# Two `xt` and value buffers, one GpSimd remainder, and another order of work in a one-core transformer layer

## The reference

```
x = x + layernorm(attention(layernorm(x)))
x = x + layernorm(ffn(layernorm(x)))

attention: Q, K, V = x W_Q + b_Q, x W_K + b_K, x W_V + b_V        (per head)
           attn = softmax(Q K^T / sqrt(64));  out = sum_h attn V W_O[h] + b_O
ffn:       gate = softmax(x gate_w^T)                              (8 experts)
           out = x weight^T + 1/16 * sum_e gate[e] * lora_V[e] (lora_U[e] x)
```

## Time and profile before

| | |
|---|---|
| median of three runs | 1090.09 us (1090.06 to 1090.18) |
| the profiled execution | 1091.16 us, span 1089.3 us |
| mean granted TensorE clock | 0.979 of full speed |
| busy | PE 94%, ScalarE 84%, VectorE 83%, GpSimd 73% of the span |
| DMA | 145 MB, 57.7% of 16 engines' time on the kernel's queue |
| instruction queues | 9 packets of 0.15 MB in all, and 10 of 0.08 MB |

### The profile page before, as it was taken

The page is one execution under the profiler, slowest core; times in us unless marked ns, Lnnn a source line. Parts: engine busy times, 40 slices in busy tenths (PEclk is TensorE's granted clock), DMA queues, the critical chain, the costliest instruction groups (busy, mean ns, idle before and its releaser), DMA issues.

```text
span 1089.3 us, 28626 instructions
## 1 busy us (share of the span) xinstructions
PE 1021.8 (94%) x8550; PEld 780.2 (72%) x8550; DVE 905.9 (83%) x1630; ACT 917.7 (84%) x3207; POOL 800.1 (73%) x778
## 2 busy tenths in 40 slices
PE   8889999999999999999999999999999999999974
PEld 7767777777777777677777777777767777777743
DVE  6888888888888888888888888888888888888841
ACT  4888888889888888888888989888988888898932
POOL 3676777787777788777778777778877777877741
PEclk9899999999999999999999999999999999999977
DMA  7364566556556556556655655755655665565570
GB/s 239 85 149 108 133 152 144 121 130 142 122 136 159 127 121 146 125 122 153 147 122 125 146 121 132 159 131 122 142 129 121 149 152 122 121 149 123 128 164 11
DMA packets 59219, 145.21 MB, mean 133 GB/s; under 512 B 17216, under 2 KB 25920, under 8 KB 59200
## 3 DMA queue, kind: packets, MB, share of 16 engines
q1 hardware_dynamic: 59200, 144.99, 57.7%
HBM read 6.50 MB, written 4.19 MB: 10 GB/s over the span
## 4 chain that ended last, share of the span: by engine, by line
PE 87%; ACT 4%; issue 3%; DVE 3%; POOL 2%; ACTq 0%; POOLq 0%; DVEq 0%
PE o_ps L460 22%; PE st_ps L438 18%; PE extra_ps L476 8%; PE qk_ps L404 8%; PE qk_ps L406 5%; PE qk_ps L405 5%; PE extra_ps L334 5%; PE extra_ps L418 4%; PE extra_ps L420 3%; PE extra_ps L419 3%; PE extra_ps L497 2%; PE extra_ps L510 2%; ACT v_sb L739 2%; ACT xt_hi L705 1%; PE extra_ps L512 1%
## 5 line engine op out<-in xcount | busy, mean ns | idle before, releaser
L1516 POOL TENSOR_TENSOR probs<-probs,inv_sum 128x1024 f32<-128x1024 f32 x256 | 486.3, 1900 | 201.4 <-DVE inv_sum L1097 201.2
L724 ACT ACTIVATE probs<-st_ps,neg_max 128x256 f32<-128x256 f32 x1024 | 477.9, 483 | 32.5 <-DVE neg_max L1089 30.2
L1089 DVE TENSOR_REDUCE neg_max<-st_ps 128x4 f32<-128x1024 f32 x256 | 310.0, 1211 | 44.7 <-PE st_ps L438 35.5
L1105 DVE STREAM_TRANSPOSE probs_b<-probs 128x1024 f32<-128x1024 f32 x256 | 313.4, 1225 | 26.8 <-POOL probs L1516 26.8
L460 PE MATMUL o_ps<-probs_t,v_sb 128*64 128x256 f32 x2048 | 253.7, 390 | 7.7 <-DVE o_lo L1113 4.3
L724 ACT ACTIVATION_READ_ACCUMULATOR probs<-st_ps,neg_max 128x1 f32 x1024 | 217.9, 213 | 0.0
L460 PEld LDWEIGHTS o_ps<-probs_t,v_sb 128*64 128x64 f32 x2048 | 136.8, 138 | 89.4 <-issue 16.0
L710 ACT CAST qk_hi<-qk_ps 128x512 fp32r<-128x512 f32 x256 | 153.5, 599 | 29.7 <-PE qk_ps L406 26.1
L438 PE MATMUL st_ps<-qk_hi 64*128 64x256 f32 x1024 | 171.9, 332 | 3.8 <-POOL qk_lo L1510 1.5
L438 PE MATMUL st_ps<-qk_lo,qk_hi 64*128 64x256 f32 x1024 | 145.2, 280 | 0.0
L1510 POOL TENSOR_TENSOR qk_lo<-qk_full,qk_hi 128x512 fp32r<-128x512 f32 x96 | 123.5, 1286 | 28.1 <-ACT qk_hi L710 14.6
(11 more groups left out here) (132 smaller groups left out, 1988.6 us busy)
## 6 DMA issues: line engine op xcount, KB each, us to landing
probs_t<-probs_b SPq DMA_DIRECT2D x1024, 128.0 KB, 2.4
out<-x_all SPq DMA_DIRECT2D x31, 128.0 KB, 1.9
x_all<-in_x SPq DMA_DIRECT2D x1, 3840.0 KB, 17.3
probs_b<-in_w_v SPq DMA_DIRECT2D x1, 512.0 KB, 4.9
probs_b<-in_w_o SPq DMA_DIRECT2D x1, 512.0 KB, 6.8
probs_b<-in_w_q SPq DMA_DIRECT2D x1, 384.0 KB, 5.3
probs_b<-in_w_k SPq DMA_DIRECT2D x1, 384.0 KB, 5.9
x_all<-in_x SPq DMA_DIRECT2D x2, 128.0 KB, 3.5
```

The source lines that it names most:

```text
L724: last = nc.scalar.activation(probs[n][:, h, j, :], st_ps[p % 2][:, (2 * h + j) * T:(2 * h + j + 1) * T], ACT.Exp, bias=neg_max[n][:, h, j ...
L1089: nc.vector.tensor_reduce(neg_max[p % N_PROBS][:, :, :].rearrange("p h j -> p (h j)"), st_ps[p % 2][:, :].rearrange("p (j s) -> p j s", j= ...
L1105: nc.vector.transpose(probs_b[chunk % 2][:, :, :, 2 * NT * n:2 * NT * (n + 1), :].rearrange("p i t n q -> p n t i q"), probs[p % N_PROBS][ ...
L1516: nc.gpsimd.tensor_tensor(probs[n][:, :, :, :].rearrange("p h j s -> p (h j) s"), probs[n][:, :, :, :].rearrange("p h j s -> p (h j) s"), ...
```

## The change

- `xt_hi`, `xt_lo` and `v_sb` have two buffers each, taken in turn by batches (`turn`, `r`). `xt_high(b)` now waits for the q, k and v products of batch b-2, and `copy_v(b, ...)` for the probabilities' products of b-2.
- `POOL_LO` is `(3,)` in place of `(1, 4, 6)`: GpSimd makes one remainder of eight in a batch, VectorE seven. There is one `qk_full` buffer in place of three, and ScalarE makes one whole copy per batch.
- To make room, `x1t` is `yt`, `ut` is `u`, `squares` are `yt` and `u`, and two constants of the set-up lie in `probs_t`. Two waits follow from it: `copy_yt` waits for `z_projected` of the batch before (in place of `y_transposed`), `apply_gate` for `variance_ready[LN_Z]` (in place of `u_transposed`).
- `run` makes loops of two batches per round, since buffer numbers must be constants. Where the number of batches is odd, one body stands ahead of the loop.
- All engines' orders are written anew, in prologue, body and epilogue.

The core of the diff:

```diff
-POOL_LO = (1, 4, 6,)
+POOL_LO = (3,)
...
-        xt_hi = sb("xt_hi", [P, T], F32R)
-        xt_lo = sb("xt_lo", [P, T], F32R)
+        xt_hi = [sb(f"xt_hi{n}", [P, T], F32R) for n in range(2)]
+        xt_lo = [sb(f"xt_lo{n}", [P, T], F32R) for n in range(2)]
...
-        qk_full_sb = {p: sb(f"qk_full{p}", [P, 2 * T]) for p in POOL_LO}
-        v_sb = sb("v_sb", [P, NT, H * DH])
+        qk_full_sb = sb("qk_full", [P, 2 * T])
+        v_sb = [sb(f"v_sb{n}", [P, NT, H * DH]) for n in range(2)]
...
-            with engine.Fori(0, high - low) as step:
-                body(step + low)
+            with engine.Fori(0, (high - low) // 2) as step:
+                for n in range(2):
+                    body(2 * step + (low + n), (low + n) % 2)
...
-                after(act, qk_projected, PAIRS * b)
-                after(act, v_projected[3], b)
+                after(act, qk_projected, PAIRS * (b - 1))
+                after(act, v_projected[3], b - 1)
...
-                after(act, o_projected, PAIRS * (b - 1) + (half + 1) * (PAIRS // 2))
+                after(act, o_projected, PAIRS * (b - 2) + (half + 1) * (PAIRS // 2))
```

## The result

The changed kernel takes 1013.91 us (median of 4 runs, 1013.4 to 1014.88) against 1090.13 of the kernel before in the same rounds (1090.06 to 1090.75): a ratio of 0.9301, 95% interval 0.9285 to 0.9317. The direction was right, the size was not.

The account below looks back on a forecast made before the run. PE and its waits were taken as the bound: 32.13 less 1.19 and 0.85, plus 0.25 leftover, gave 30.35 us per batch; 29 batches -50.1, ends +1.1, so 1041 us, 4.5% faster, range 1030 to 1067.

Parts of the forecast that it names:

- Waits at the seam: Between two loop batches, PE's waits at the transpose of xn (0.76) and first query product (0.43) vanish: gain 1.1 to 1.19 us.
- Changes of kind: In PE's loop order, 22 switches between product kinds become 20 (0.4 us), three fp32 pieces get shorter (0.45): 0.85 per batch.
- the 1054 by that rule alone: Kernel time in us if only tiling-mode changes drain TensorE, without the 0.45 for fp32 pieces: batch 0.45 longer.
- Leftover waits of 0.25 a batch: In the loop, remaining PE waits given several close margins: 0.25 us added, 30.35 us per batch (30.1 to 30.7).
- Remainders moved: Per loop batch, two of three GpSimd remainders go to VectorE: ScalarE 27.5, GpSimd 22.3, VectorE 29.0 to 29.2 us busy.
- Blocks, shared tiles, the loop: In the loop, DMA transfers stay hidden, waits from shared tiles cost nothing, and the two-batch branch costs 0 (at most 4 us).
- Ends: Before batch 3's transpose +0.6 us (-3 to +4); behind scores 6 of batch 31 +0.5 us (-2 to +2).
- A: Rival: VectorE sets the loop's pace; 31.2 us per batch, 1066 us, if half its idle time stays; chance 0.13.
- B: Rival: loop code is fetched anew each round, 56 to 160 us in 14 rounds, kernel 1098 to 1200; chance 0.10.
- C: Rival: gain given back at the ends or by the DMA; 10 us more, 1051, if the first batches run badly; chance 0.07.
- D: Rival: PE's 1.19 us of waits only move to x1's transposes or scores 3; 31.3 per batch, 1068 us; chance 0.10.

Follow-up runs that it names:

- e1: Changed kernel with scores 6 ahead of the last value quarter again in the loop: period 31.11 us (+1.18), one run of 1048.85 us.
- e2: Changed kernel with the products with probabilities 6 and 7 ahead of the transpose of xn in the loop: period 30.58 us (+0.66), one run of 1031.25 us.
- e3: Changed kernel with scores 1 moved between q/k 2 and q/k 3, two more changes of kind per batch: period 30.30 us (+0.38), one run of 1022.16 us.
- e7: Changed kernel with one more unused VectorE reduction (about 0.6 us) per loop batch: period 30.32 us (+0.39), single run of 1028.72 us.
- e8: Changed kernel with two more unused VectorE reductions (about 1.2 us) per loop batch: period 30.90 us (+0.98), single run of 1040.45 us.
- e5: Kernel before with one remainder on GpSimd and seven on VectorE, PE's order and buffers as before: 1103.67 us, ratio 1.012 to the kernel before.
- e6: Changed kernel with the loops written out as straight code for all 32 batches: 1011.47 us, ratio 0.9289, period 29.93 us.
- e15: Changed kernel with the old order of set-up and batch 0, but GpSimd's order left as changed: 1020.91 us, ratio 0.9379, batch 3's transpose at 99.5 us.
- e12: Changed kernel with batch 2's transpose, first projections and first values behind scores 7 of batch 1 again, loop untouched: 1026.35 us, ratio 0.9426.
- e4: Changed kernel with one buffer for xt_hi and xt_lo in place of two: period 29.92 us, one run of 1018.53 us.
- e10: Changed kernel with value quarters 1 to 3 of batch 1 and the transpose of batch 2 moved back in the prologue: 1014.72 us, ratio 0.9299.
- e9: Kernel before with 26 small unused products where PE waits in its prologue: 1091.46 us, ratio 1.0009.
- e11: Changed kernel with the old order of set-up and first batch on four engines, GpSimd's remainder of pair 3 behind the scaling of pair 1: 1028.66 us.
- e13: Changed kernel with another end: last block transfers issued from two queues, two PSUM banks for attention, second group ahead of batch 30's gate: 1009.46 us, ratio 0.9269.

## Why the prediction was wrong, step by step

**Waits at the seam: right, 0.13 too small.** Forecast -1.1 to -1.19, and they are gone (no bracket in the timeline, e1 and e2 bring them back). The size was read from the column of idle time. PE's starts say more. Before (a value quarter, scores 6 and the last value quarter ahead of a seam, then the scores behind it):

```profile
521.94 0.50 PE L418 MATMUL extra_ps<-wv_hi,xt_hi 128*128 128x512 f32 x1
522.84 0.38 PE L438 MATMUL st_ps<-qk_hi 64*128 64x256 f32 x2
523.74 0.50 PE L418 MATMUL extra_ps<-wv_hi,xt_hi 128*128 128x512 f32 x1
...
525.81 0.39 PE L438 MATMUL st_ps<-qk_hi 64*128 64x256 f32 x2
```

A value quarter takes 0.90 from its start to the next kind's, the one ahead of the transpose 1.71 (523.74 to 525.45), so the wait costs 0.81. Scores take 0.90 (522.84 to 523.74), those ahead of the query product 1.41 (525.81 to 527.22), so that wait costs 0.51. Together 1.32 and not 1.19.

**Changes of kind: right.** What is left is 32.13 - 1.32 - 29.92 = 0.89, against 0.85. e3 measures 0.19 per change apart from all else, and the fp32 pieces with a query product behind them are shorter as forecast: transpose of `u` 0.19 in place of 0.37, of `yt` 0.19 in place of 0.34, z 0.89 (507.46 to 508.35) in place of 1.09. The 0.89 a batch is a remainder of the sum; these rows alone give 0.4 and 0.53. The Trainium skill's drain rule ("TensorEngine Tiling (Array Packing)", Key Properties) agrees with the first of these numbers and is silent on the second; the 1054 by that rule alone is ruled out for this kernel.

**Leftover waits of 0.25 a batch: wrong, they are 0.** With the 0.13 and the 0.04 above, and rounding, this makes the 0.43 between 30.35 and 29.92, 12.5 us in 29 batches. I saw margins of 0.1 to 0.6 and added a quarter of a microsecond for caution, with no row behind it. PE is busy for 29.92 of 29.92. e7 and e8 show that the caution was close to being right: VectorE has 0.2 to spare.

**Remainders moved: right, loads as forecast.** VectorE 28.8 to 29.2, ScalarE 26.9, GpSimd 22.2 to 22.7. e5 shows that this part alone gives next to nothing in the loop (-0.10) while PE's order is the old one. Whether the new order needs it is open: it was not run with three remainders on GpSimd.

**Blocks, shared tiles, the loop: right, nothing in the loop.** PE never waits there for blocks. e6 puts the loop itself at nothing measurable.

**Ends: the step that failed most.** Forecast +0.6 before the transpose of batch 3, from -3 to +4; measured -11.9. I treated the start as the old straight code with two more remainders on a VectorE that was 94% busy from 40 to 75 us, and priced only what is added. But the diff rewrites the straight code as well. VectorE idled 22 of 107.6 us before (12.7 of 95.7 after), all but 2 of it outside the window of 40 to 75 that I rested on. 1.9 of the 11.9 are the products that moved behind, as forecast. The new order of the set-up is worth about 4 (e15), and pulling batch 2's transpose, projections and values three to six groups ahead the rest (e12), both as what putting the old piece back costs, and both with a part of the clock in them. The second `xt` buffer has its share in this (e4: 3 us in one profile with a half-speed stretch at 59.9 to 63.3). Early values alone (e10) and half speed in the start of the kernel before (e9) don't explain it. Behind scores 6 of batch 31 I forecast +0.5 and it was -3.1. Nearly all of that is the clock, for which the forecast had no term. PE stands still there as long as before (21.5 us against 21.8), but it is busy for 26.9 us in place of 29.6 although it has more products (183 against 165), at a granted clock of 0.81 in place of 0.71: before the last serial chain half speed was granted for 6.8 us (973.3 to 980.1), in the kernel before for 17.1 (1046.2 to 1063.3). From the last transpose of `xn` to the end the variants with an untouched end take 76.6 to 82.8 us, the shortest (e2, e6) with 3.4 us at half speed ahead of that chain and the longest (e7, e10, e11) with 20.4.

**The rivals.** A did not happen: VectorE follows PE, though with 0.2 us to spare. B is excluded by the packets (14 and 15 on the two queues, none in 770 us of loop) and by e6. Of the two statements of the Trainium skill that were weighed there ("Runtime: NRT & Kernel Launch", Instruction fetch mechanics), the trace agrees with the buffer sizes: from the third round on no taken branch of a two-batch body brings a packet. C came with the other sign. D did not happen: no wait of PE appears at `x1` or scores 3.

## What to carry to other kernels

Straight code ahead of a loop is a kernel of its own: when a change rewrites it, lay it out like the loop, above all where the next batch's first projections start, because that is when the busiest helper engine runs dry. Here three batches of start gave 12 us and 29 batches of loop 63. Read what a wait costs from the starts of PE's groups, with the wait and without it, and not from the idle column: the column is missing the step to the next product (1.19 against 1.32). And don't add an allowance for waits that no row shows; put it in the range. Look at the DMA engines' share before adding a second issuing queue: here it was 91% already, and the queue gained 0.4 us.

## What the runs showed of the hardware that was not expected

- PE's granted clock at the ends differs between executions of nearly the same code: half speed (1.2 GHz) at 34.6 to 38.0 in the changed kernel's profile, at 34.0 to 40.9 in e8's, not again in the starts of e6's and e13's, with the transpose of batch 3 at 95.7, 96.1, 92.6 and 93.2. The instructions ahead of 34 us are the same in all four, and full speed (2.4 GHz) was first granted at 7.3, 6.7, 5.6 and 5.2. So a forecast of an end can't be sharper than about 3 us.
- Two issuing queues don't make two streams. 32 issues took 17.0 us from two queues and 21.7 from one, but where both issued at once the landing time of both rose, to 4.8 and 5.0 us against 2.4, and the DMA engines' share was 101% against 91%.
- Issues on ScalarE's queue ran beside its own exponentials: three issues of 0.61 to 0.66 us stand in the trace at 965.3 to 967.2, inside four exponentials that kept their 0.48 to 0.49 us.
- A body with some 1,140 instructions on PE and 275 on ScalarE ran 12 of its 14 rounds without a packet of code; the last packets of the loop come at 195 us, in the second round.
